# Attention outputs turned in 32x32 blocks on VectorE instead of whole on TensorE, with the sum and the scaling on GpSimd

## The chip, the core and the metric

The kernel is one launch on one core of a Trainium2 chip. The metric is the device time of that launch in microseconds (us), as the median over several runs. The core's engines work side by side, each through its own list of instructions in order: TensorE (PE in the profile; its weight loads are PEld), VectorE (DVE), ScalarE (ACT), GpSimd (POOL) and SyncE (SP), which here does nothing but issue DMAs. They wait for each other on counting semaphores.

## The reference

The input x is (4, 2048, 256) in fp32: four batches of 2048 tokens. Between two expert layers stands windowed attention with 16 heads of 16 columns:

```
x = x + 0.5 * ffn(layernorm(x))
x = x + attention(layernorm(x))          # |q - k| <= 128, or q == 0, or k == 0
x = x + 0.5 * ffn(layernorm(x))

attention:  softmax(q k^T / 4, masked) v, heads joined, @ Wo^T
ffn:        top-2 of 8 experts; an expert whose token count exceeds
            capacity 1280 contributes nothing
```

With these inputs every expert exceeds its capacity, so that the kernel computes the routing counts, finds no expert to run, and skips both expert layers. What is timed is the attention over all four batches and the routing.

## The kernel before, in words

**Tiles.** A batch is 16 tiles of 128 tokens; its 16 heads are 4 head groups of 4 heads. A group (16 tiles x 4 heads) is the outer unit: 16 groups, n = 0 to 15, four for each batch. A *step* is one tile of one group, 256 in all; a *quarter* is one head of a step. `stages` gives every piece of work a quarter number, `schedule` makes one list of events from these, and each engine walks the same list in order, doing its own events. The constants `QK_AT`, `OUT_AT`, `LATE_AT`, `MAX_AT` and the like are those quarter numbers. No planner is involved; the order is fixed when the kernel is built.

**What a quarter does.** Event A (L934): TensorE multiplies queries and keys over the window into one of three PSUM banks `a_ring`; VectorE (L1431) adds the mask and takes the row maximum. Event B runs 20 steps behind A: TensorE multiplies again with the maxima subtracted (L962), ScalarE takes the exponential into `probs` (L1105), GpSimd zeroes the two corners of the band (L1218, L1223, event CUT), and TensorE multiplies by the values (L980, event PV) into the bank `o_bank`.

**Stacks.** Queries and keys are split in three bf16 pieces (`pieces`, L1055, L1070, L1206). For each group and each quarter of its tiles (chunk c = 0 to 3) SyncE issues 12 DMAs, STACK (L718, L721), which place the pieces in `q_stack` and `k_stack`. TensorE's A event of tiles 0, 3, 7 and 11 waits until the stack of chunk 0, 1, 2, 3 has landed:

```
if h == 0 and t in (0, 3, 7, 11):
    i = 4 * g + (t + 1) // 4
    pe.wait_ge(stack_sem(i), stacked(i))
```

`pieces` has two buffers: ScalarE's first piece of chunk i (L1053) waits for the landing of the stack of chunk i - 2.

**The end of a group.** After its last tile the maxima are turned and split (TURN_MAX, MAX, PIECES), and SyncE issues 3 DMAs (MAX, L727) which put them in `q_stack`. GpSimd (P0, L1195) and ScalarE (EXP0, L1095) compute `p0`, the weight of key 0 for every query. With group n ending at quarter 64(n+1), the DMAs of SyncE are put at: MAX +2, STACK of the next group's chunk 2 at +11, of chunk 3 at +27, and those of the group after it, chunk 0 at +43 and chunk 1 at +59 (batches 1 to 3; the first batch has its own numbers).

**The outputs.** `o_bank` holds for four tiles (a quartet) the sums with heads on partitions (head h at partitions 32h, 17 columns of values and weight sum) and tokens in the row. There are 64 quartets. ScalarE copies it to `o_raw` (COPY_OUT, L1122; VectorE, L1352, for the last six), TensorE turns it by 16 small matmuls against columns of the identity (TURN, L1000), VectorE adds the term of key 0 in PSUM (OUT_ADD, L1460), takes reciprocals (L1467) and multiplies into `attn` (L1478), tokens on partitions. The term of key 0, `glob_term`, is made by GpSimd (GLOB, L1235).

**The projection.** For each quarter of a batch (LATE), TensorE turns the rows of `attn` by transposes of 128x128 (TURN_ATTN, L792), in two halves; ScalarE copies them to `attnT` (L1046; VectorE, L1344, in the last batch), and TensorE multiplies by Wo (PROJECT, L806).

Of the kernel before, what the change touches and what calls it, by code (L numbers as in the profile page):

```python
# [7 lines left out]
ALU = mybir.AluOpType  # L8
# [5 lines left out]
H, HD = 16, 16  # L14
# [34 lines left out]
def build(nc, x, wqk, wback, wv, wo, gate, w1, b1, w2, b2, consts, x1, out):  # L49
    ctx = ExitStack()  # L50
    with ctx:
        def sb(name, shape, dt=FP32):
# [28 lines left out]
        v0_all = sb("v0_all", [P, H * VW])  # L81
        o_raw = sb("o_raw", [P, 4 * P])
        glob_term = sb("glob_term", [P, 4, HG, VW])
        recip = sb("recip", [P, 4, HG])
        s0T = sb("s0T", [P, NT, H])
        row_max = sb("row_max", [P, 2, HG, NT])
        p0_arg = sb("p0_arg", [P, NT, HG])
        p0 = sb("p0", [P, 2, NT, HG])
# [12 lines left out]
        o0_norm = sb("o0_norm", [1, H, HD])  # L101
# [6 lines left out]
        attn_flat = attn[:, :, :].rearrange("p t d -> p (t d)")  # L108
        probs_flat = probs[:, :, :, :].rearrange("p a h n -> p (a h n)")
# [6 lines left out]
        o0_row = arena[0:1, 512:512 + H * VW]  # L116
# [4 lines left out]
        take = ident.rearrange("p (h c) -> p h c", c=SP)[:, :, 0:VW]  # L121
# [22 lines left out]
                 "glob_ready", "o_added", "recip_ready", "stored", "stored0", "stored1", "stored2",  # L144
# [248 lines left out]
        LATE = {'LOAD': -6, 'TURN_ATTN': 1, 'PROJECT': ((7, 8, 10, 10), (12, 12, 14, 14)),  # L393
                'BASE': 0, 'MOMENTS': (12, 17, 19, 21), 'RSTD': 23, 'STORE': 19}
        OUT_AT = (0, 0, 3, 3, 0, -1, -1, 0, 2, -1, 1, 0, 0, 0, 3, 4)
        OUT = {'TURN': 0, 'ADD': 0, 'RECIP': 1, 'MULT': 1}
        MAX_AT = {'KEY0': -1, 'TURN_MAX': 1, 'MAX': 2, 'PIECES': 3, 'P0': -1, 'EXP0': 6}

        def stages(nb, first):
# [22 lines left out]
            for i, (phase, b, c, at) in enumerate(order):  # L422
                plan = EARLY if phase == "EARLY" else LATE
                end(at + plan["LOAD"] if b or phase == "LATE" else -96, "LOAD", i)
                if phase == "LATE":
                    for p in range(2):
                        begin(at + LATE["TURN_ATTN"], "TURN_ATTN", i, p)
                        opening(at + LATE["TURN_ATTN"] + 1, "TURN_ATTN_IN", i, p)
# [20 lines left out]
            for n in range(NG * nb):  # L449
# [21 lines left out]
                opening(at + MAX_AT["EXP0"], "EXP0", n)  # L471
                for q in range(4):
                    at = 4 * LAG_TURN + GROUP * n + 16 * q + OUT_AT[4 * g + q]
                    begin(at + OUT["TURN"], "TURN", 4 * n + q)
                    end(at + OUT["ADD"], "OUT_ADD", 4 * n + q)
                    end(at + OUT["RECIP"], "OUT_RECIP", 4 * n + q)
                    end(at + OUT["MULT"], "OUT_MULT", 4 * n + q)
# [38 lines left out]
        FILLS = ("XT", "TURN_ATTN", "PROJECT", "QK", "TURN_MAX", "TURN", "VALUES", "FIRST", "FOLD")  # L516
        PARTED = ("PROJECT", "QK", "VALUES", "FIRST")
        EMPTIED = {"XT_IN": "XT", "TURN_ATTN_IN": "TURN_ATTN", "PROJECT_IN": "PROJECT", "REST": "QK", "PIECES": "TURN_MAX",
# [46 lines left out]
        def attend(nb, dram, batch_at, tiles_at, first):  # L565
# [42 lines left out]
            def drained(kind, n):  # L608

                if kind == "COPY_OUT":  # L610
                    return 4 * n + 3 + LAG_PV > NT * NG * nb
# [969 lines left out]
```

## Time and profile before

| | us |
|---|---|
| median of 3 runs | 870.6 |
| lowest, highest | 869.64, 871.29 |
| profiled execution, first to last instruction (span) | 867.2 |
| busy: TensorE matmul, its weight load | 814.6, 606.9 |
| busy: VectorE, ScalarE, GpSimd | 758.3, 637.2, 488.1 |
| mean granted TensorE clock, share of full | 0.997 |

The profile is of one execution; besides its span no time of its own is recorded. The profile counts an engine as busy in the union of its instructions. Matmuls overlap each other, so that the start of one to the start of the next is shorter than either lasts. SyncE has no busy time in the page: its DMA issues stand in the timeline of its queue (SPq), where the length is the time for which the queue was held by the issue, and a separate figure tells when the data landed.

### The profile page before, as it was taken

What the parts mean: (1) busy time and instruction counts of PE and PEld (TensorE: products, weight loads), DVE (VectorE), ACT (ScalarE), POOL (GpSimd) and SP (SyncE); (2) the same over time, 40 slices, a digit from 0 to 9 for tenths busy, and PEclk for the clock granted to TensorE, in tenths of its full rate; (3) what the DMA queues carried; (4) which work ended last, traced back from release to release, by engine and by line L of the source; (5) the groups of instructions that cost most, each with busy time, mean ns of one, the idle gap of its engine ahead of it and who ended that gap; (6) DMA issues with size and microseconds to landing.
All of it is one profiled execution on the core that took longest, in us unless ns stands there. A gap on an engine that the chain in (4) does not pass through costs nothing. (4 is left out here: it accounts for less than half of the span.)

```text
span 867.2 us, 50607 instructions
## 1 busy us (share of the span) xinstructions
PE 814.6 (94%) x21504; PEld 606.9 (70%) x21505; DVE 758.3 (87%) x2819; ACT 637.2 (73%) x1417; POOL 488.1 (56%) x874
## 2 busy tenths in 40 slices
PE   9798999999999999999999999898999999999894
PEld 8555667767777777667778777666778777766572
DVE  7898899989887899998987899998988889998785
ACT  2268888897877667998877666898777766888850
POOL 3212556675555557765554465675554556656763
PEclk9999999999999999999999999999999999999998
DMA  7722224432212344441213335352222335220113
GB/s 231 116 81 75 67 73 121 135 88 70 77 62 96 111 146 119 120 127 62 89 51 101 106 105 161 108 131 71 74 73 68 106 93 149 94 77 18 49 51 102
DMA packets 93191, 83.51 MB, mean 96 GB/s; under 512 B 17568, under 2 KB 92192, under 8 KB 92960
## 3 DMA queue, kind: packets, MB, share of 16 engines
q1 hardware_dynamic: 91360, 78.91, 30.1%
q8 instruction: 171, 2.80, 1.5%
q10 hardware_dynamic: 1600, 1.31, 1.0%
q14 instruction: 60, 0.49, 0.2%
HBM read 20.66 MB, written 8.39 MB: 33 GB/s over the span
## 5 line engine op out<-in xcount | busy, mean ns | idle before, releaser
L1105 ACT ACTIVATE probs<-bank 128x384 f32<-128x384 f32 (+1 forms) x1024 | 462.8, 480 | 146.8 <-PE bank L962 137.4
L1431 DVE CUSTOM_DVE_ANT_0 bank<-bank,con 128x288 f32<-128x288 f32 x1024 | 494.4, 518 | 53.2 <-PE bank L934 44.8
L934 PE MATMUL bank<-k_stack,q_stack 96*32 96x288 bf16 x4096 | 325.4, 288 | 10.7 <-DVE row_max L1431 5.7
L962 PE MATMUL bank<-q_stack,k_stack 99*32 99x288 bf16 (+2 forms) x4096 | 319.8, 285 | 16.0 <-ACT probs L1105 9.7
L980 PE MATMUL bank<-probs,v_sb 128*32 128x128 f32 x5888 | 305.4, 272 | 3.6 <-issue 1.5
L1218 POOL TENSOR_SCALAR_AFFINE_SELECT probs<-probs 128x512 f32<-128x512 f32 x240 | 154.8, 645 | 180.1 <-ACT probs L1105 179.5
L980 PEld LDWEIGHTS bank<-probs,v_sb 128*32 128x32 f32 x5888 | 192.1, 110 | 36.7 <-issue 5.3
L962 PEld LDWEIGHTS bank<-q_stack,k_stack 99*32 99x32 bf16 x4096 | 123.6, 95 | 79.7 <-ACT probs L1105 53.5
L934 PEld LDWEIGHTS bank<-k_stack,q_stack 96*32 96x32 bf16 x4096 | 127.3, 95 | 74.0 <-DVE row_max L1431 21.3
L1223 POOL TENSOR_SCALAR_AFFINE_SELECT probs<-probs 128x512 f32<-128x512 f32 x240 | 154.1, 642 | 19.3 <-ACT probs L1105 19.2
L823 PE MATMUL bank<-xnT,wqk_sb 128*32 128x256 f32 x2048 | 158.1, 379 | 0.6 <-DVE neg_max L1453 0.5
L1431 DVE DVE_READ_ACCUMULATOR2_ANT row_max<- 128x1 f32 x1024 | 144.1, 141 | 0.0
L1206 POOL TENSOR_TENSOR pieces<-rest,pieces 128x512 bf16<-128x512 f32 x64 | 74.4, 1162 | 61.7 <-ACT pieces L1070 61.5
L838 PE MATMUL bank<-wv_sb,xnT 128*32 128x272 f32 x1024 | 83.9, 393 | 1.7 <-ACT v_sb L1077 1.1
L806 PE MATMUL bank<-wo_sb,attnT 128*32 128x264 f32 x1024 | 72.0, 386 | 1.9 <-DVE x_ring L1339 0.9
L823 PEld LDWEIGHTS bank<-xnT,wqk_sb 128*32 128x32 f32 x2048 | 64.6, 110 | 5.6 <-ACT v_sb L1077 1.2
L1055 ACT ACTIVATE pieces<-bank 128x512 bf16<-128x512 f32 x64 | 38.3, 599 | 20.7 <-PE bank L823 19.5
L1359 DVE TENSOR_TENSOR rest<-bank,pieces 128x512 f32<-128x512 f32 x64 | 44.1, 688 | 4.3 <-ACT pieces L1055 4.1
L1266 DVE BATCH_NORM_STATS2 stats<-x_ring 128x6 f32<-128x256 f32 x112 | 47.1, 421 | 0.2
L1000 PE MATMUL bank<-con,o_raw 128*32 128x68 f32 x2048 | 44.4, 223 | 2.6 <-issue 1.7
L1070 ACT ACTIVATE pieces<-rest 128x512 bf16<-128x512 f32 x64 | 40.6, 635 | 8.0 <-DVE rest L1359 7.8
L806 PEld LDWEIGHTS bank<-wo_sb,attnT 128*32 128x32 f32 x1024 | 33.2, 109 | 13.4 <-issue 2.2
(126 smaller groups left out, 737.2 us busy)
## 6 DMA issues: line engine op xcount, KB each, us to landing
q_stack<-pieces SPq DMA_DIRECT2D x384, 64.0 KB, 2.7
k_stack<-pieces SPq DMA_DIRECT2D x364, 64.0 KB, 2.7
x_ring<-in_x SPq DMA_DIRECT2D x28, 512.0 KB, 4.5
out_x<-x_ring SPq DMA_DIRECT2D x16, 512.0 KB, 3.9
attn<-in_x SPq DMA_DIRECT2D x4, 512.0 KB, 6.0
wback_sb<-in_wback SPq DMA_DIRECT2D x8, 256.0 KB, 6.0
k_stack<-pieces ACTq DMA_DIRECT2D x20, 64.0 KB, 3.6
q_stack<-neg_max SPq DMA_DIRECT2D x48, 16.0 KB, 2.3
```

What stands on the lines that cost most here:

```text
L806: last = pe.matmul(bank_of("PROJECT", i, t)[SP * s:SP * (s + 1), 0:D + E], attnT[:, t // 2, k, at:at + SP], wo_sb[:, k, :], start=(k == 0) ...
L823: last = pe.matmul(bank_of("QK", g, c)[SP * s:SP * (s + 1), 256 * half:256 * (half + 1)], wqk_sb[:, g % NG, k, SP * s:SP * (s + 1)], xnT[: ...
L838: last = pe.matmul(bank_of("VALUES", b, t)[SP * s:SP * (s + 1), 0:D + HD], xnT[:, k, at:at + SP], wv_sb[:, k, :], start=(k == 0), stop=(k ...
L934: last = pe.matmul(a_ring[i % len(a_ring)][SP * s:SP * (s + 1), 0:WIN], q_stack[g % 2][0:KROWS, h, q:q + SP], k_stack[g % 2][0:KROWS, h, q ...
L962: last = pe.matmul(b_ring[i % len(b_ring)][SP * s:SP * (s + 1), start:final], k_stack[g % 2][0:SROWS, h, WINDOW + P * j + SP * s:WINDOW + ...
L980: last = pe.matmul(o_bank[SP * h:SP * (h + 1), P * (i % 4):P * (i % 4 + 1)], v_sb[:, j, VW * head:VW * head + SP], probs[:, j % 4, h, P * ...
L1105: act.activation(probs[:, j % 4, h, c0:c1], b_ring[i % len(b_ring)][:, c0:c1], ACT.Exp, scale=LOGIT_SCALE).then_inc(S["exp_ready"], 1)
L1206: pool.tensor_tensor(pieces[i % 2][:, 2, :], rest[:, :], pieces[i % 2][:, 1, :], ALU.subtract).then_inc(S["piece3_ready"], 1)
L1218: pool.affine_select(out=part, in_=part, compare_op=ALU.is_ge, fill=0.0, base=0, pattern=[[0, HG], [1, P]], channel_multiplier=-1).then_in ...
L1223: pool.affine_select(out=part, in_=part, compare_op=ALU.is_ge, fill=0.0, base=0, pattern=[[0, HG], [-1, P]], channel_multiplier=1).then_in ...
L1266: dve.bn_stats(stats[:, t, :], x_tiles(i)[:, t, :]).then_inc(S["stats_ready"], 1)
L1431: dve.tensor_tensor_reduce(out=a_ring[i % len(a_ring)][:, 0:WIN], in0=a_ring[i % len(a_ring)][:, 0:WIN], in1=mask, scale=1.0, scalar=con[: ...
```

## The change

1. `o_raw` is turned by VectorE, `dve.transpose`, in 32x32 blocks, into `o_turned` in SBUF (OUT_TURN, 58 of the 64 quartets). For the last six VectorE turns `o_bank` directly, and the copy goes. TensorE's TURN goes.
2. After a turn in blocks, partition 32h + r holds token r of each block of 32 for head h: heads stay on groups of 32 partitions. So `v0_all` (FIRST stage 6) and the first row (stage 8) are made in that layout, by four matmuls in place of one.
3. `p0` must be moved to the same layout. SyncE issues 16 DMAs of 32 partitions x 16 values for each group (P0_IN, at quarter +8 after the group's end), between MAX (+2) and the next STACK (+11). GLOB waits for these, and is put one step later, 36 quarters after the group's end.
4. OUT_ADD and OUT_MULT go to GpSimd (from SBUF); OUT_RECIP stays on VectorE, between them.
5. TensorE's TURN_ATTN and ScalarE's copy go: VectorE turns `attn`, in its new layout, straight to `attnT`, in 32x32 blocks. The rows of Wo are loaded in that order, by 4 DMAs in place of 1.

```diff
-        OUT = {'TURN': 0, 'ADD': 0, 'RECIP': 1, 'MULT': 1}
-        MAX_AT = {'KEY0': -1, 'TURN_MAX': 1, 'MAX': 2, 'PIECES': 3, 'P0': -1, 'EXP0': 6}
+        OUT = {'TURN': 0, 'ADD': 1, 'RECIP': 5, 'MULT': 6}
+        OUT_END = {'TURN': 0, 'ADD': 0, 'RECIP': 1, 'MULT': 1}
+        P0_MOVES = HG * P // SP
+        MAX_AT = {'KEY0': -1, 'TURN_MAX': 1, 'MAX': 2, 'PIECES': 3, 'P0': -1, 'EXP0': 6, 'P0_IN': 8}
...
-        LATE = {'LOAD': -6, 'TURN_ATTN': 1, 'PROJECT': ((7, 8, 10, 10), (12, 12, 14, 14)),
+        LATE = {'LOAD': -6, 'TURN_ATTN': (2, 5), 'PROJECT': ((7, 8, 10, 10), (12, 12, 14, 14)),
...
+                        elif kind == "P0_IN":
+                            g, = n
+                            sp.wait_ge(S["p0_ready"], g + 1)
+                            if g >= 2:
+                                sp.wait_ge(S["glob_ready"], 4 * (g - 1))
+                            for h in range(HG):
+                                for m in range(P // SP):
+                                    sp.dma_start(p0_heads[SP * h:SP * (h + 1), g % 2, m, :],
+                                                 p0[SP * m:SP * (m + 1), g % 2, h, :]).then_inc(S["p0_moved"], 16)
...
-                        elif kind == "TURN":
-                            n, = n
-                            pe.wait_ge(S["o_copied"], n + 1)
-                            claim(pe, "TURN", n)
-                            for i in range(4):
-                                for s in range(4):
-                                    at = P * i + SP * s
-                                    last = pe.matmul(
-                                        bank_of("TURN", n)[SP * s:SP * (s + 1), HG * VW * i:HG * VW * (i + 1)],
-                                        o_raw[:, at:at + SP], take, start=True, stop=True)
-                            last.then_inc(full_sem("TURN", n), 1)
...
+                        elif kind == "OUT_ADD":
+                            n, = n
+                            pool.wait_ge(S["o_turned"], n + 1)
+                            pool.wait_ge(S["glob_ready"], n + 1)
+                            sums = o_turned[:, :, :, 0:VW].rearrange("p t m c -> p (t m) c")
+                            pool.tensor_tensor(sums, sums, glob_term[:, :, :, :].rearrange("p t m c -> p (t m) c"),
+                                               ALU.add).then_inc(S["o_added"], 1)
+                        elif kind == "OUT_MULT":
...
+                            pool.wait_ge(S["recip_ready"], n + 1)
...
+                        elif kind == "TURN_ATTN":
...
+                            dve.transpose(attnT[:, p, :, :],
+                                          attn_heads[:, at:at + 8, :, :].rearrange("p b k e -> p k b e"))\
+                               .then_inc(S["attn_turned"], 1)
+                        elif kind == "OUT_TURN" and not drained(n[0]):
+                            n, = n
+                            dve.wait_ge(S["o_copied"], n + 1)
+                            if n:
+                                dve.wait_ge(S["out_ready"], n)
+                            dve.transpose(o_turned[:, :, :, :].rearrange("p t m c -> p (t m c)"), o_raw[:, :])\
+                               .then_inc(S["o_turned"], 1)
```

## Rows read from the trace of the kernel before

**Rows 1.** The page, busy time and share of the span of each engine.

```profile
PE 814.6 (94%) x21504; PEld 606.9 (70%) x21505; DVE 758.3 (87%) x2819; ACT 637.2 (73%) x1417; POOL 488.1 (56%) x874
```

**Rows 2.** Busy time by stretch: tile 7 to the end, of groups 8 to 11.

```profile
core 0: us, PE busy (x) PEld busy (x) DVE busy (x) ACT busy (x) POOL busy (x), PEclk, DMA share, GB/s
...
420.30:449.80 29.50, 29.50 (x821) 23.38 (x817) 25.17 (x93) 23.17 (x53) 15.97 (x25) 1.00 0.24 77
...
471.10:505.20 34.10, 34.09 (x893) 25.25 (x887) 28.46 (x105) 23.49 (x52) 17.60 (x33) 1.00 0.35 111
...
528.60:556.90 28.30, 25.66 (x740) 19.42 (x728) 26.52 (x108) 21.47 (x48) 20.41 (x39) 1.00 0.51 148
...
576.30:605.60 29.30, 26.02 (x800) 19.34 (x792) 24.80 (x97) 25.30 (x58) 17.50 (x30) 1.00 0.34 91
```

**Rows 3.** Timeline of SyncE's queue from group 7's MAX (start us, us held, what).

```profile
404.91 1.78 SPq L727 DMA_DIRECT2D q_stack<-neg_max  x3
406.79 1.08 SPq L718 DMA_DIRECT2D q_stack<-pieces  x1
407.91 0.59 SPq L721 DMA_DIRECT2D k_stack<-pieces  x1
408.55 0.59 SPq L718 DMA_DIRECT2D q_stack<-pieces  x1
...
416.38 0.59 SPq L718 DMA_DIRECT2D q_stack<-pieces  x1
```

**Rows 4.** The same queue: last DMA of chunk 2's stack, groups 9 to 11.

```profile
462.07 0.60 SPq L718 DMA_DIRECT2D q_stack<-pieces  x1
...
519.62 1.40 SPq L718 DMA_DIRECT2D q_stack<-pieces  x1
...
570.23 1.64 SPq L718 DMA_DIRECT2D q_stack<-pieces  x1
```

**Rows 5.** Timeline of TensorE: A of tile 7, groups 8 to 11, and one TURN.

```profile
420.27 0.30 PE L934 MATMUL bank<-k_stack,q_stack 96*32 96x288 bf16 x4
...
420.68 0.66 PE L1000 MATMUL bank<-con,o_raw 128*32 128x68 f32 x32
421.16 0.31 PE L934 MATMUL bank<-k_stack,q_stack 96*32 96x288 bf16 x4
...
471.15 0.33 PE L934 MATMUL bank<-k_stack,q_stack 96*32 96x288 bf16 x2
...
528.58 0.29 PE L934 MATMUL bank<-k_stack,q_stack 96*32 96x288 bf16 x4
...
576.27 0.30 PE L934 MATMUL bank<-k_stack,q_stack 96*32 96x288 bf16 x4
```

**Rows 6.** DMAs of the page, with median us from issue to landing.

```profile
q_stack<-pieces SPq DMA_DIRECT2D x384, 64.0 KB, 2.7
...
out_x<-x_ring SPq DMA_DIRECT2D x16, 512.0 KB, 3.9
```

**Rows 7.** Line L733, the stores: ns held, minimum/median/maximum, and starts.

```profile
L733 SPq DMA_DIRECT2D out_x<-x_ring x16: 383/390/1317, 291.7 to 858.7; - x16
```

**Rows 8.** Timeline of ScalarE: EXP0 of group 7.

```profile
406.53 0.25 ACT L1095 ACTIVATE p<-p_arg 128x64 f32<-128x64 f32 x1
```

**Rows 9.** Groups of instructions: count, busy us, mean ns of one, idle before.

```profile
L1206 POOL TENSOR_TENSOR pieces<-rest,pieces 128x512 bf16<-128x512 f32 x64 | 74.4, 1162 | 61.7 <-ACT pieces L1070 61.5
...
L1000 PE MATMUL bank<-con,o_raw 128*32 128x68 f32 x2048 | 44.4, 223 | 2.6 <-issue 1.7 <-ACT o_raw L1122 0.9
...
L1235 POOL TENSOR_TENSOR glob_term<-v_all,p 128x272 f32<-128x272 f32 x64 | 41.4, 647 | 1.8 <-DVE v_all L1400 1.8
...
L1460 DVE TENSOR_TENSOR bank<-bank,glob_term 128x272 f32<-128x272 f32 x64 | 29.2, 456 | 10.2 <-PE bank L1000 9.1
...
L1478 DVE TENSOR_TENSOR attn<-bank,recip 128x256 f32<-128x256 f32 x64 | 27.2, 425 | 3.3
...
L792 PE MATMUL bank<-con,attn 128*128 128x128 f32 x128 | 17.4, 279 | 0.8 <-DVE attn L1478 0.3
...
L1352 DVE COPY o_raw<-bank 128x512 f32<-128x512 f32 x6 | 4.1, 687 | 5.4 <-PE bank L980 5.4
```

More of the change, by code:

```diff
@@ L471, in stages @@
                 opening(at + MAX_AT["EXP0"], "EXP0", n)
+                end(at + MAX_AT["P0_IN"], "P0_IN", n)
                 for q in range(4):
                     at = 4 * LAG_TURN + GROUP * n + 16 * q + OUT_AT[4 * g + q]
[L474 to L477, printed above, removed]
+                    plan = OUT if n < NG * nb - 1 else OUT_END
+                    opening(at + plan["TURN"], "OUT_TURN", 4 * n + q)
+                    end(at + plan["ADD"], "OUT_ADD", 4 * n + q)
+                    end(at + plan["RECIP"], "OUT_RECIP", 4 * n + q)
+                    end(at + plan["MULT"], "OUT_MULT", 4 * n + q)
             for b in range(nb):
@@ L515, in build @@
         FIRST_PARTS = (4, 4, 4, 1, 1, 1, 1, 4, 1)
[L516 removed]
+        FILLS = ("XT", "PROJECT", "QK", "TURN_MAX", "VALUES", "FIRST", "FOLD")
         PARTED = ("PROJECT", "QK", "VALUES", "FIRST")
[L518 to L519 removed]
+        EMPTIED = {"XT_IN": "XT", "PROJECT_IN": "PROJECT", "REST": "QK", "PIECES": "TURN_MAX",
+                   "VALUES_IN": "VALUES", "FIRST_IN": "FIRST", "FOLD_IN": "FOLD"}
         def schedule(nb, first):
@@ L542, in schedule @@
                     events.append(("CUT", b))
[L543 removed]
+                q, turn = divmod(k + 2 - LAG_TURN, 4)
                 if turn == 0 and 0 <= q < items // 4:
@@ L899, in _ @@
                                 claim(pe, "FIRST", b, stage)
-                                last = pe.matmul(m[:, 0:H * VW], ones[0:1, :], v_sb[0:1, 0, 0:H * VW],
-                                                 start=True, stop=True)
+                                rows = v_heads[0:1, 0, 0:H, :].rearrange("p (g h) c -> p g h c", h=HG)
+                                for h in range(HG):
+                                    last = pe.matmul(m[SP * h:SP * (h + 1), 0:NG * VW], ones[0:1, 0:SP], rows[:, :, h, :],
+                                                     start=True, stop=True)
                             elif stage == 7:
@@ L914, in _ @@
                                 claim(pe, "FIRST", b, stage)
-                                last = pe.matmul(m[0:1, 0:H * VW], ones[:, 0:1], masked_o0,
-                                                 start=True, stop=True)
+                                rows = masked_o0.rearrange("p (g h c) -> p g h c", h=HG, c=VW)
+                                for h in range(HG):
+                                    last = pe.matmul(m[SP * h:SP * (h + 1), 0:NG * VW], ones[:, 0:SP], rows[:, :, h, :],
+                                                     start=True, stop=True)
                             if part == FIRST_PARTS[stage] - 1:
@@ L1116, in _ @@
                             act.activation(wide[1], wide[0], ACT.Exp).then_inc(S["route_exp"], 1)
-                        elif kind == "COPY_OUT" and not drained(kind, n[0]):
+                        elif kind == "COPY_OUT" and not drained(n[0]):
                             n, = n
```

174 lines of the change are left out of this document (72 added, 102 removed).

## Prediction

> **What bounds the kernel now.** I read the page first. TensorE is busy 94% of the span, VectorE 87%, ScalarE 73%, GpSimd 56% [rows 1]. No engine is idle long enough to say at once what an edit is worth, so I went to the busy time by stretch. In the second part of a group (tile 7 to the next group's start), group 8 and group 9 have TensorE busy in every microsecond (29.5 of 29.5, 34.1 of 34.1) with VectorE at 25.2 and 28.5; in group 10 VectorE leads (26.5 of 28.3, TensorE 25.7); in group 11 three engines are close (TensorE 26.0, VectorE 24.8, ScalarE 25.3 of 29.3) [rows 2]. So TensorE sets the pace in half of the loop and shares it in the rest. Relief of TensorE alone is worth something, but VectorE is close behind.
>
> The engines are not all there is. SyncE's queue has its own timeline. From MAX on it issues DMA behind DMA: starts at 407.91 and 408.55 are 0.64 us apart, of which the queue is held 0.59 [rows 3], and there are 12 of them for each stack, 48 for a group; one group takes about 51 us (A of tile 7 starts at 420.27 and, a group later, at 471.15 [rows 5]). Some issues take longer: the first of chunk 2's stack starts at 406.79 and the last, held for 0.59, at 416.38, 10.2 us for twelve against 7.6 at 0.64 each [rows 3]. What the stacks are for, and when, is the next thing to see. Chunk 2's stack of group 8 is issued last at 416.38, lands 2.7 us after that by the median [rows 3, 6], at 419.1, and A of tile 7, which waits for it, starts at 420.27 [rows 5]. The spare is 1.2 us. For groups 9, 10 and 11, reckoned in the same way (2.1 us from the end of the issue to the landing): landed 464.8, 523.1, 574.0, needed 471.15, 528.58, 576.27, spare 6.4, 5.5 and 2.3 [rows 4, 5, 6]. The mean of four is 3.9 us. This queue is the hidden third bound: it costs nothing now, and it has little left.
>
> **The change, part by part.**
>
> *TensorE* loses TURN and TURN_ATTN. One TURN is 0.66 long, but the next matmul starts 0.48 after it [rows 5]; 64 of these are 31 us. TURN_ATTN is 17.4 busy in all [rows 9], taken whole. Together 48 us (62 if the busy time of TURN, 44.4, were taken [rows 9]). The new FIRST stages add 6 small matmuls for a batch, nothing against that.
>
> *VectorE* loses OUT_ADD 29.2 and OUT_MULT 27.2 [rows 9] and 14 copies of 0.69 (six of o_raw, eight of attnT, priced by the former's row), 9.6: 66 us. It gains 58 + 6 + 32 = 96 turns of 128x512. The trace has no turn on VectorE. The nearest row is a copy of the same size, 0.687 [rows 9], and I take it: 66 us. Bounds: no cheaper than the smaller OUT_MULT, 0.425 (25 us less); at the dear end a turn that takes two passes, 1.37 (66 us more). Net nothing: VectorE stays at 758.
>
> *ScalarE* loses 24 copies of attnT, a little under 0.7 each, some 16 us. It leads nowhere in rows 2, so this is hidden.
>
> *GpSimd* gains 64 adds of 128x272 at 0.647 (its GLOB is that shape) and 64 products of 128x256, half of its 1.162 for 512 columns or 0.6 [rows 9]: 41 + 38 = 79, which makes 567 of 867 us. It has 8 to 16 us idle in each stretch of rows 2, so the work itself is hidden. What is not quite hidden is the order: VectorE's reciprocal now waits for GpSimd's add, and whatever A follows it on VectorE waits too. The add stands 4 quarters, about 3 us, ahead of it, behind two band cuts. I price this at 0 and bound it by one add each, 64 x 0.65 = 41 us.
>
> *SyncE* gains 16 moves of p0 for each group, and this is the step that decides. They wait for EXP0, which ends at 406.8 [rows 8], just when MAX's three issues end (404.91 + 1.78) [rows 3]: no further wait, but no gap to hide in. Then 16 issues at 0.64 are 10.2 us. Behind them in the same queue is the stack of chunk 2, with a spare of 1.2 to 6.4 us. It lands 10.2 later; A of tile 7 comes 10.2 - 3.9 = 6.3 us late in the mean. TensorE works in order, so nothing behind that A runs, B and its exponentials stop with it, and VectorE, 87% busy, has no A to do. MAX of this group comes as much later, so that the next group meets the same delay again: it doesn't amortise. It happens to 15 groups (the last one's moves have no stack behind them, and GLOB, 28 quarters after them, is not reached): 15 x 6.3 = 95 us. In the first batch the stacks have other places; I take the same mean.
>
> The price of one issue is bounded below by the cheapest DMA this queue shows, a store of median 0.390 [rows 7], plus the 0.04 between issues: 6.9 for 16, 3.0 late, 45 us in all. Above, by what the twelve of group 8 took, long issues included, 10.2/12 = 0.85: 13.6, 9.7 late, 146 us. I take 0.64, as the moves touch few bytes, and bytes don't seem to matter (those cheapest stores have 512 KB [rows 6]).
>
> The Trainium skill, page "DMA: Bandwidth & Descriptors", section "Anatomy of one DMA", lists the sequencer's dispatch of a DMA (there for those that GpSimd issues) at about 50 ns. By that the 16 moves would cost an estimated 0.8 us, under every spare above, and the whole term would be zero. The rows of this queue hold 0.59 for nearly each DMA, so I follow them; that rule is the fast rival below.
>
> *What TensorE's relief is worth beside it.* Work saved ahead of tile 7 only makes the wait for the stack longer. In the part after tile 7, three of a group's four TURNs are saved, 1.4 us, and in the second group of a batch four halves of TURN_ATTN as well, 4 x 0.54 = 2.2. Where TensorE alone leads (groups 8, 9) all of it counts, where it shares (10, 11) half: 1.4 + 3.6 + 0.7 + 0.7 = 6.4 for a batch, 25 for four.
>
> *Sum.* 867.2 + 95 - 25 = 937 us of span. The median of the runs is 3.4 above the span of the profiled execution, so 941 us.
>
> **The rivals.**
>
> *The moves are hidden* (other side). If an issue of such a small move is cheap, every stack lands in time. Then TensorE's relief counts before tile 7 too: per batch 1.9 + 4.1 in the two groups that it leads, and half of 1.9 + 2.2 and of 1.9 in the others, 9 us, 36 for four: 835. The deciding point: the late A costs nothing on balance while 16 moves take less than the spare, 3.9, plus 25/15 = 1.7 us, that is 0.35 us a move. For it: all rows of 0.59 are of two kinds of DMA, MAX and STACK [rows 3], and may owe it to their shapes. Against it: no DMA of this queue, of any shape, is under 0.383 [rows 7].
>
> *Turns on VectorE are dear, or its reciprocal waits for GpSimd*, on top of the late stacks. Two-pass turns add 66 us of VectorE's time; in the stretches where it has 3 to 5 us of room most of it vanishes, in those like group 10's it doesn't; I count half, 33: 974.
>
> *Hidden moves, dear turns or waits.* 835 plus 33: 868, no measurable change. It needs two things at once.
>
> *ScalarE stalls earlier than TensorE.* Its first piece of the next group's chunk 0 reuses the buffer of chunk 2 and waits for the same landing; in the second and third group of a batch it is placed 3 to 5 quarters ahead of A of tile 7. At 0.8 us a quarter (50.9/64) this adds up to 3 us in half of the groups: 15 to 20 us, 959. It is inside the range and not in the sum, since ScalarE has room.
>
> *The change doesn't do what it says.* TensorE's turns are gone from its list for certain; there is no such rival.
>
> **How the numbers follow.** Late stacks as summed, with the bounds of the issue price (891 to 992) and of ScalarE: 0.72. Late stacks with dear turns or waits: 0.14. Moves hidden, TensorE's relief kept: 0.10. Both small: 0.04. The predicted time is the first, 941. The range of 8 in 10 is 885 to 985: it leaves out the hidden moves and the far end of the dear cases. Runs of this kernel agree within about 0.2%, so a change below that can't be told from none: slower by more 0.87, within it 0.03, faster by more 0.10.
>
> **What would show it.** Right: SyncE's queue shows 16 issues of p0_heads at about 0.64 right behind each MAX; TensorE's A (L934 before) waits for the DMA of k_stack or q_stack, some 6 us, 15 times; from one A of tile 7 to the next it takes some 5 us more; GpSimd near 567 busy, VectorE near 758, both with a lower share. Wrong in the first step if the moves are held under 0.35 each or TensorE doesn't wait for stacks; wrong in the price of a turn if VectorE's transposes are far from 0.69; wrong in the order if VectorE's reciprocal shows idle time ended by GpSimd's add.

## The result, and the profile after

The changed kernel takes 1003.0 us by the median (999.18 to 1004.25), the kernel before 870.1 on the same chip: a ratio of 1.151, 95% interval 1.147 to 1.155. The profiled execution has a span of 997.6 us against 867.2. The forecast was 941, with a range of 885 to 985: right in direction and in the main mechanism, 62 us too low and outside the range.

The busy line of the page after and its row of granted clock in 40 slices (before in [rows 1]):

```profile
PE 810.3 (81%) x19376; PEld 570.3 (57%) x19377; DVE 753.8 (76%) x2785; ACT 627.2 (63%) x1393; POOL 574.2 (58%) x1002
...
PEclk9899898999797997989799898988989799897998
```

No engine has more to do in a way that could matter: VectorE has 4.5 us less, GpSimd 86 more and is still idle 42% of the span. All shares fell, TensorE's from 94% to 81%. The time went into gaps in which everything stands. SyncE's queue after, from group 7's MAX on (start, us held, what; before in [rows 3]):

```profile
467.77 1.89 SPq L737 DMA_DIRECT2D q_stack<-neg_max  x3
469.76 11.49 SPq L746 DMA_DIRECT2D p_heads<-p  x16
481.35 0.59 SPq L728 DMA_DIRECT2D q_stack<-pieces  x1
...
488.66 0.59 SPq L728 DMA_DIRECT2D q_stack<-pieces  x1
```

The sixteen moves stand between MAX and chunk 2's stack, as forecast, and hold the queue for 11.5 us. TensorE in the same stretch (in brackets: idle before, and what ended it; before in [rows 5]), and the busy time of all engines in slices of 5 us (columns as in [rows 2]):

```profile
482.45 0.60 PE L829 MATMUL bank<-xnT,wqk_sb 128*32 128x256 f32 x8
491.29 0.43 PE L944 MATMUL bank<-k_stack,q_stack 96*32 96x288 bf16 x4 [8.24 <-DMA q_stack<-pieces]
```

```profile
480.00:485.00 5.00, 2.92 (x72) 1.70 (x72) 3.86 (x17) 3.16 (x8) 3.30 (x6) 1.00 0.17 52
485.00:490.00 5.00, 0.00 (x0) 0.00 (x0) 0.00 (x0) 0.00 (x0) 0.47 (x1) 0.62 0.29 101
490.00:495.00 5.00, 3.71 (x60) 2.55 (x64) 1.72 (x7) 1.30 (x3) 0.00 (x0) 0.50 0.32 105
495.00:500.00 5.00, 5.00 (x112) 3.39 (x108) 4.25 (x17) 4.04 (x9) 3.12 (x5) 0.86 0.22 72
500.00:505.00 5.00, 5.00 (x148) 4.10 (x142) 4.15 (x16) 4.27 (x11) 2.97 (x6) 1.00 0.26 85
```

The list of waits names the same cause, once on ScalarE and once on TensorE, with the total in us, the count and the longest; the third row is the wait that was bounded by 41 us and priced at nothing:

```profile
ACT pieces L1045 <- DMA q_stack<-pieces: 70.7, 10, 9.4
...
PE bank L944 <- DMA q_stack<-pieces: 64.7, 8, 10.6
...
DVE recip L1487 <- POOL o_turned L1236: 6.5, 6, 1.8
```

Last, the groups of instructions that are new or moved (count, busy us, mean ns of one, idle before):

```profile
L1236 POOL TENSOR_TENSOR o_turned<-o_turned,glob_term 128x272 f32<-128x272 f32 x64 | 45.9, 718 | 2.5 <-DVE o_turned L1372 2.4
...
L1247 POOL TENSOR_TENSOR attn<-o_turned,recip 128x256 f32<-128x256 f32 x64 | 41.5, 648 | 21.3 <-DVE recip L1487 20.9
...
L1372 DVE STREAM_TRANSPOSE o_turned<-o_raw 128x512 f32<-128x512 f32 x58 | 41.0, 707 | 1.4 <-ACT o_raw L1112 1.2
...
L1364 DVE STREAM_TRANSPOSE attnT<-attn 128x512 f32<-128x512 f32 x32 | 22.3, 698 | 0.3
```

**Where the 130 us of span are.** From each trace I took, for the 15 groups with a next one, the time from the first issue of MAX to the A of tile 7, and from there to the next MAX; beside them the first A, the four batches (from a batch's first A to the next batch's) and what follows the last A. For these last three the mark is VectorE's instruction of event A, some 0.5 us behind TensorE's, so the first A stands 0.5 us later in the table than in the rows of TensorE. For group 7 after, the first is 467.8 to 491.3, 23.5 us; before it was 404.9 to 420.3, 15.4 [rows 3, 5].

| kernel | first A at | batches 1 to 4 | MAX to A of tile 7, sum | A of tile 7 to MAX, sum | tail |
|---|---|---|---|---|---|
| before | 26.9 | 175.1, 200.4, 203.1, 190.6 | 257.3 | 474.0 | 71.1 |
| after | 31.9 | 198.0, 235.3, 235.3, 224.7 | 366.4 | 487.9 | 72.5 |
| e1_no_moves | 30.6 | 178.9, 197.5, 196.4, 185.5 | 254.9 | 462.7 | 72.2 |
| e2_moves_alone | 27.0 | 204.2, 242.0, 242.3, 233.9 | 373.2 | 509.6 | 70.6 |
| e3_half_moves | 31.3 | 190.1, 212.3, 212.5, 205.0 | 302.2 | 478.4 | 71.3 |
| e5_bounce_wo_late | 26.9 | 182.5, 198.1, 196.8, 187.2 | 253.4 | 472.7 | 72.4 |
| e7_kept_busy | 31.0 | 200.4, 238.5, 236.3, 230.5 | 393.1 | 473.2 | 72.5 |
| e9_kept_fit | 33.3 | 201.3, 232.0, 233.3, 224.6 | 369.5 | 481.1 | 71.3 |
| e10_one_wo | 26.9 | 181.2, 197.3, 199.1, 188.5 | 254.6 | 471.9 | 72.0 |
| e11_back_late | 27.7 | 175.9, 197.0, 196.7, 185.4 | 253.9 | 463.6 | 74.7 |

After less before: +109.1 from MAX to A, +13.9 from there to MAX, +5.0 ahead of the first A, +1.4 in the tail, together 129 of 130. The 109 fall on 13 of the 15. In the first and third group of the first batch the moves stand behind chunk 2's stack and the stop comes at chunk 3 instead: 36.1 and 36.0 where before had 30.5 and 30.5. That is 11 of the 13.9, so all stops together are 120 us, 8.0 for each of 15.

### The profile page after: what moved, and what is told of

Same layout as the page of the kernel before. It is cut to its first block and busy times, and to the rows that moved or that the text cites. A ratio compares the mean times of both kernels' runs of the same rounds, so it can differ in the third digit from the quotient of the medians.

```text
span 997.6 us, 46656 instructions
## 1 busy us (share of the span) xinstructions
PE 810.3 (81%) x19376; PEld 570.3 (57%) x19377; DVE 753.8 (76%) x2785; ACT 627.2 (63%) x1393; POOL 574.2 (58%) x1002
## 5 line engine op out<-in xcount | busy, mean ns | idle before, releaser
L944 PE MATMUL bank<-k_stack,q_stack 96*32 96x288 bf16 x4096 | 329.6, 300 | 89.3 <-DMA q_stack<-pieces 64.7
L972 PE MATMUL bank<-q_stack,k_stack 99*32 99x288 bf16 (+2 forms) x4096 | 326.7, 296 | 69.0 <-ACT probs L1095 64.6
L990 PE MATMUL bank<-probs,v_sb 128*32 128x128 f32 x5888 | 314.0, 281 | 9.4 <-POOL probs L1212 5.3
L829 PE MATMUL bank<-xnT,wqk_sb 128*32 128x256 f32 x2048 | 162.6, 389 | 0.6 <-DVE neg_max L1482 0.5
L844 PE MATMUL bank<-wv_sb,xnT 128*32 128x272 f32 x1024 | 88.7, 412 | 1.6 <-ACT v_sb L1067 1.1
L812 PE MATMUL bank<-wo_sb,attnT 128*32 128x264 f32 x1024 | 74.4, 402 | 3.4 <-DVE attnT L1364 2.1
L1247 POOL TENSOR_TENSOR attn<-o_turned,recip 128x256 f32<-128x256 f32 x64 | 41.5, 648 | 21.3 <-DVE recip L1487 20.9
L1060 ACT ACTIVATE pieces<-rest 128x512 bf16<-128x512 f32 x64 | 40.5, 633 | 12.9 <-DVE rest L1386 12.8
L1236 POOL TENSOR_TENSOR o_turned<-o_turned,glob_term 128x272 f32<-128x272 f32 x64 | 45.9, 718 | 2.5 <-DVE o_turned L1372 2.4
```

Of the source, the lines that this page charges most:

```text
L812: last = pe.matmul(bank_of("PROJECT", i, t)[SP * s:SP * (s + 1), 0:D + E], attnT[:, t // 2, k, at:at + SP], wo_sb[:, k, :], start=(k == 0) ...
L829: last = pe.matmul(bank_of("QK", g, c)[SP * s:SP * (s + 1), 256 * half:256 * (half + 1)], wqk_sb[:, g % NG, k, SP * s:SP * (s + 1)], xnT[: ...
L844: last = pe.matmul(bank_of("VALUES", b, t)[SP * s:SP * (s + 1), 0:D + HD], xnT[:, k, at:at + SP], wv_sb[:, k, :], start=(k == 0), stop=(k ...
L944: last = pe.matmul(a_ring[i % len(a_ring)][SP * s:SP * (s + 1), 0:WIN], q_stack[g % 2][0:KROWS, h, q:q + SP], k_stack[g % 2][0:KROWS, h, q ...
L972: last = pe.matmul(b_ring[i % len(b_ring)][SP * s:SP * (s + 1), start:final], k_stack[g % 2][0:SROWS, h, WINDOW + P * j + SP * s:WINDOW + ...
L990: last = pe.matmul(o_bank[SP * h:SP * (h + 1), P * (i % 4):P * (i % 4 + 1)], v_sb[:, j, VW * head:VW * head + SP], probs[:, j % 4, h, P * ...
```

## The experiments

Four questions were put: is it the moves, and all of it (e1, e2, e3)? Can they be had more cheaply or elsewhere (e4, e6, e12)? What else does the change cost (e5, e8, e10)? What is lost behind a stop (e7, e9)? The times that open each measurement are medians; ratios are to the kernel before on the same chip (872.1 us for e1 to e4, 871.6 for e5 to e8, 871.9 for e9 to e12), with 95% intervals. Spans, windows and sums by group come from one profiled execution of each kernel.

### e1_no_moves: the change without the moves

```diff
-                end(at + MAX_AT["P0_IN"], "P0_IN", n)
...
+                            pool.memset(p0_heads[:, :, :, :], 0.0).then_inc(S["p0_moved"], 1)
...
-                            pool.wait_ge(S["p0_moved"], 16 * P0_MOVES * (g + 1))
+                            pool.wait_ge(S["p0_ready"], g + 1)
```

> The changed kernel without its 256 moves of p0: GpSimd reads a block of zeros in their place, so the term of key 0 is left out of the sums; every other instruction stays. Late stacks (my theory): SyncE's queue is as free as before, no A waits for a stack, TensorE's clock stays full, and the time falls from 1003 to 840 to 865 us (835 for TensorE's relief, plus the 5 us by which the first A came later). Rival, the work on GpSimd and VectorE and the waits between them cost the time: it stays above 960 us.

Measured: 866.6 us against 872.1, ratio 0.993 (0.990 to 0.996), 1.6 above the range. The span is 861.1. All the added time hangs on the moves: from e1 to after they cost 136.5 us of span. The rest of the change helps, by 6 us rather than the 25 to 36 that I had reckoned. Its page and the windows of tile 7 to the next group, groups 8 to 11 (before in [rows 2]; these start and end at TensorE's A, so they are up to 1.1 us shorter at the end):

```profile
PE 782.6 (91%) x19376; PEld 558.7 (65%) x19377; DVE 749.0 (87%) x2785; ACT 624.5 (73%) x1393; POOL 573.0 (67%) x1003
```

```profile
424.70:452.00 27.30, 27.30 (x703) 20.25 (x699) 23.69 (x86) 22.61 (x53) 19.20 (x30) 1.00 0.25 83
473.60:505.10 31.50, 30.13 (x754) 20.74 (x749) 28.22 (x104) 21.15 (x48) 20.57 (x36) 1.00 0.35 115
529.10:555.20 26.10, 23.91 (x608) 16.53 (x609) 24.98 (x101) 20.23 (x44) 22.82 (x42) 1.00 0.51 152
575.70:602.20 26.50, 23.46 (x677) 16.94 (x673) 23.03 (x88) 24.43 (x56) 21.18 (x36) 1.00 0.31 88
```

TensorE leads in the first window only, full; in the second it now has 1.4 us idle with VectorE at 28.2 of 31.5. By the page TensorE's busy time fell 32 us (814.6 to 782.6), where I had taken 48.

### e2_moves_alone: the kernel before, plus the moves

Nothing reads the moved data.

```diff
+        p0_heads = sb("p0_heads", [P, 2, P // SP, NT])
...
+                end(at + MAX_AT["P0_IN"], "P0_IN", n)
...
+                            for h in range(HG):
+                                for m in range(P // SP):
+                                    sp.dma_start(p0_heads[SP * h:SP * (h + 1), g % 2, m, :],
+                                                 p0[SP * m:SP * (m + 1), g % 2, 4 * h:4 * h + 4, :].rearrange("p t h -> p (t h)")).then_inc(S["p0_moved"], 16)
```

> The kernel before with the 16 moves for each group added at the same place of SyncE's queue, into a buffer that nothing reads; nothing else of the change. Late stacks: the moves hold the queue for 11.7 us a group against a mean spare of 3.9, so 15 x 7.8 = 117 us and some 2 us a group for the half clock after each stop: 990 to 1025 us. Rival, the moves are not what costs: below 890 us.

Measured: 1021.4 us, ratio 1.168 (1.162 to 1.174), inside the range; span 1019.9: the moves alone cost 153 us. The waits are those of the changed kernel:

```profile
PEld bank L946 <- DMA q_stack<-pieces: 68.4, 8, 10.9
ACT pieces L1067 <- DMA q_stack<-pieces: 68.1, 10, 9.5
```

By the table the 153 are 115.9 from MAX to A, 35.6 from A to MAX (15.8 of it stops at chunk 3, 38.4 twice against 30.5; 19.8 spread over the other stretches), and 1 elsewhere. The stops are 132, 8.8 for each of 15, and 20 are lost *behind* them. Sixteen moves take 12.1 us here in the mean of the 15 groups, so the spare that the stops leave is 3.3. Given the moves, the rest of the change takes 22 us off (997.6 against 1019.9): 29 in the batches, less 7 ahead of the first A and in the tail. Of the 29, 6.8 lie from MAX to A of tile 7 (373.2 against 366.4), where the stack sets the time and not TensorE.

### e3_half_moves: eight moves a group

Heads 2 and 3 are not moved.

```diff
-                            for h in range(HG):
+                            for h in range(2):
```

> The changed kernel with the moves of two of the four heads only, 8 a group; the other two heads' key 0 term is zero. Late stacks: 8 moves hold the queue for 5.9 us, which is 2 over the mean spare and less than the spare in half of the groups, so most of the 15 stops shrink to 0 to 5 us: 880 to 915 us, much nearer to the kernel without moves than halfway. A cost in proportion to the moves would give some 925.

Measured: 923.0 us, ratio 1.058 (1.053 to 1.063), outside the range and near the 925 that I had named for a cost in proportion to the moves. The expectation came from my forecast's arithmetic: 8 moves less a spare of 3.9 should leave little. They hold the queue for 5.74 us in this row of the queue's timeline, and chunk 2's stack starts 7.7 us behind MAX in that group, where it started 1.9 behind it before [rows 3], 5.8 later:

```profile
438.08 5.74 SPq L746 DMA_DIRECT2D p_heads<-p  x8
```

The span is 922.5, 55 over the kernel before. Of these, 45 us stand from MAX to A in the 15 groups (302.2 against 257.3) and 5.3 at one chunk 3 (35.8 against 30.5). The spare that these groups really have, delay of the queue less delay of A, is 2.2, 0.4, 5.6 and 2.1 for groups 8 to 11 (5.8 less 3.6, 5.4, 0.2 and 3.7), a mean of 2.6. Group 9, which I had given 6.4, has next to none. Its stop is on ScalarE. This is ScalarE's timeline in the changed kernel at the same group, where the wait is longer:

```profile
538.94 0.49 ACT L1095 ACTIVATE probs<-bank 128x384 f32<-128x384 f32 x1 [0.41 <-PE bank L972]
547.96 0.60 ACT L1045 ACTIVATE pieces<-bank 128x512 bf16<-128x512 f32 x1 [8.52 <-DMA q_stack<-pieces]
```

The first piece of the next group's chunk 0 waits for the landing that frees its buffer, 5 us ahead of A of tile 7 (552.9), and the exponentials queued behind it wait too. The second groups of batches 2 to 4 are alike in the changed kernel: MAX to A of tile 7 grew by 10.7, 10.0 and 10.9 us in groups 5, 9 and 13, no less than where TensorE itself waits, though the stack that TensorE needs had over 5 us of spare there before.

### e4_bounce: one DMA out to DRAM, four back

```diff
+        MAX_AT = {'KEY0': -1, 'TURN_MAX': 1, 'MAX': 2, 'PIECES': 3, 'P0': -1, 'EXP0': 6, 'P0_IN': 8, 'P0_BACK': 12}
...
+                            sp.dma_start(p0_dram[g % 2, :, :, :].rearrange("p h t -> p (h t)"),
+                                         p0[:, g % 2, :, :].rearrange("p h t -> p (h t)")).then_inc(S["p0_out"], 16)
...
+                            by_head = p0_dram[g % 2, :, :, :].rearrange("(m r) h t -> h r m t", r=SP)
                             for h in range(HG):
+                                sp.dma_start(p0_heads[SP * h:SP * (h + 1), g % 2, :, :], by_head[h])\
+                                  .then_inc(S["p0_moved"], 16)
```

> The changed kernel with p0 moved through DRAM: one DMA of all 128 partitions out, ahead of the stack of chunk 2, and four DMAs back (one for each head), behind that stack. 5 issues a group for 16, of which only one (0.7 us) stands before the urgent stack; the four (2.9 us) delay the stack of chunk 3, whose spare is 2.8 us at the least. Late stacks: 845 to 870 us, within 15 of the kernel without moves. Rival: above 960 us.

Measured: 877.0 us, ratio 1.005 (1.002 to 1.007), 7 above the range. SyncE's queue:

```profile
458.74 1.78 SPq L738 DMA_DIRECT2D q_stack<-neg_max  x3
460.77 0.38 SPq L745 DMA_DIRECT2D p_scratch<-p  x1
461.25 1.17 SPq L729 DMA_DIRECT2D q_stack<-pieces  x1
...
470.44 3.02 SPq L754 DMA_DIRECT2D p_heads<-p_scratch  x4
```

The same 32 KB cost the queue 0.4 us ahead of the stack in place of 11.5, and the stops are gone (253.5 from MAX to A). So it is the issues and not the bytes: five take 3.4 us in this group where sixteen took 11.7 in the mean, and four of the five stand behind the urgent stack. How much of the gain is their number and how much their place this run doesn't separate; e6 shows that the place alone isn't enough. What stayed above the expectation asked for something outside the groups, and the first A showed it (next run).

### e5_bounce_wo_late: e4, and Wo's four loads later

The change also loads Wo head by head in four DMAs of 64 KB, ahead of the first stack. Here they come at quarter 80.

```diff
-                        by_head = wo.rearrange("(g h c) k n -> h g c k n", g=2, h=HG)
-                        for h in range(HG):
-                            sp.dma_start(wo_sb[SP * h:SP * (h + 1), :, 0:D], by_head[h]).then_inc(S["wo_in"], 16)
...
+                end(80, "WO_IN")
```

> The kernel with p0 moved through DRAM (877 us), and the four loads of Wo issued at quarter 80 in place of before the first stack. Each of them has a slowest dimension of 2 and so, by my reading, few DMA engines work on 256 KB just when the first stack is to land; the first A came 3.7 to 5 us later in every kernel with these loads, and not in the kernel before. If so, the first A is back at 27 us and the time falls by 4 to 7: 870 to 873 us. Rival, the new layout's first matmuls or VectorE's work in the opening delay it: no change, 877.

Measured: 870.6 us against 871.6, ratio 0.9995 (0.997 to 1.002), inside the range. The first A of TensorE in the timelines of after and of this run (e4, which differs from this run in the loads alone, has it at 30.93):

```profile
31.29 0.67 PE L944 MATMUL bank<-k_stack,q_stack 96*32 96x288 bf16 x8 [7.35 <-DMA k_stack<-pieces]
```

```profile
26.40 0.55 PE L954 MATMUL bank<-k_stack,q_stack 96*32 96x288 bf16 x8 [2.01 <-DMA k_stack<-pieces]
```

Four loads placed ahead of the first stack make it land 4.5 to 5 us late. The queue isn't what delays it: the first issue of that stack starts at 16.52 after and at 16.48 before. It is the data that lands later. The forecast has no term for them: I had read the diff's DMAs inside the loop and not those ahead of it.

### e6_moves_behind: the moves behind chunk 2's stack

```diff
-        MAX_AT = {'KEY0': -1, 'TURN_MAX': 1, 'MAX': 2, 'PIECES': 3, 'P0': -1, 'EXP0': 6, 'P0_IN': 8}
+        MAX_AT = {'KEY0': -1, 'TURN_MAX': 1, 'MAX': 2, 'PIECES': 3, 'P0': -1, 'EXP0': 6, 'P0_IN': 12}
```

> The changed kernel with its 16 moves at quarter +12 in place of +8, behind the stack of chunk 2. If only the place in the queue counts, chunk 3's stack (spare 2.8 to 10 us) is now 11.7 us late: stops of 2 to 9 us, some 6 in the mean, 950 to 985 us. If the queue is short of time in all (some 70 DMAs at 0.73 us are 51 us, as long as a group), moving them about gains little and the time stays above 980.

Measured: 971.2 us, ratio 1.115 (1.109 to 1.120), inside the range. From MAX to A is 252.4 now, as without moves; from A to MAX 570.1, 96 more than before. TensorE waits as long at a time, at the next chunk:

```profile
PE bank L944 <- DMA q_stack<-pieces: 49.4, 12, 11.9
```

Neither of the two places tried has 11 us free: 48 stack issues and 3 for MAX already take 33 of a group's 51 us at 0.64 each, and more with the long ones. Moves spread over several places of the group, a few at each, were not tried.

### e7_kept_busy: idle matmuls in the stops

Up to 30 matmuls of ones are put ahead of A of tile 7's wait, into a free bank of `a_ring`.

```diff
+        KEPT = (0, 0, 30, 0, 30, 0, 22, 28, 30, 0, 22, 28, 30, 0, 22, 28)
...
+                            if h == 0 and t == 7 and KEPT[g]:
+                                i = HG * n + h
+                                pe.wait_ge(S["a_free"], i - len(a_ring) + 1)
+                                for _ in range(KEPT[g]):
+                                    pe.matmul(a_ring[i % len(a_ring)][:, 0:P], ones[:, :], ones[:, :], start=True, stop=True)
```

> The changed kernel, with TensorE given 22 to 30 idle matmuls of 128x128 (some 6 to 8 us) ahead of the wait for chunk 2's stack in the ten groups where it stops there for 7 to 11 us. The stops stay as long. If the half clock behind each stop costs 2 to 3 us, as the longer stretches behind tile 7 say, the granted clock is back over 0.96 and the time falls by 15 to 30 us, to 973 to 990. If the clock costs nothing, since VectorE sets the pace behind a stop: no change, 1000 to 1005.

Measured: 1009.1 us, ratio 1.157 (1.152 to 1.162): missed, slower than the changed kernel. The mean granted clock rose from 0.922 to 0.948 and the stretches behind the stops shrank by 14.7, but those ahead grew by 26.7, of which 20 are in groups 6, 10 and 14 (26.8, 26.2 and 26.0 became 32.8, 32.8 and 33.2): there the idle matmuls came on top of the stop, as ScalarE's wait ends it and not TensorE's. These three groups hide what the clock does; e9 leaves them out.

### e9_kept_fit: the same, fitted to the stops

```diff
+        KEPT = (0, 0, 30, 0, 30, 0, 0, 24, 26, 0, 0, 26, 26, 0, 0, 30)
```

> e7_kept_busy again, with idle matmuls only in the seven groups whose stop stands at this wait in full (24 to 30 of them, 6.6 to 8.3 us); in e7_kept_busy those of groups 6, 10 and 14 came on top of the stop and cost 6 to 7 us each. In the others its groups were 1.2 to 2.6 us shorter than the changed kernel's. If that is the half clock: 7 x 2 = 14 us off 1003, 985 to 995. If it was chance: 1000 to 1005.

Measured: 1001.2 us, ratio 1.149 (1.144 to 1.154), which can't be told from the changed kernel's 1.151; it is the "chance" branch of the expectation. The mean clock is 0.946. The stretches behind the stops are 6.8 shorter, those ahead 3.1 longer, the first A is 1.4 later. The groups show more than the total. The first 5 us from A of tile 7 of group 8, in the changed kernel and in this one (columns as in [rows 2]):

```profile
491.29:496.29 5.00, 5.00 (x76) 3.26 (x80) 2.27 (x9) 2.15 (x5) 0.56 (x1) 0.50 0.31 103
```

```profile
493.44:498.44 5.00, 5.00 (x136) 3.92 (x136) 4.41 (x16) 4.01 (x9) 1.60 (x3) 1.00 0.31 104
```

At a granted clock of 1.00 TensorE gets through 136 matmuls in place of 76, and VectorE and ScalarE are at work at once. From A of tile 7 to MAX this group takes 32.7 us after, 30.2 here and 30.3 in e1, which has no stop. In the four treated groups that have the full clock in these first 5 us (2, 4, 7 and 8) the stretches sum to 125.3 after, 121.7 here and 122.0 in e1. In the three that have 0.66 to 0.68 (11, 12 and 15) it is 87.3, 85.4 and 84.0. So the half clock is what makes the stretch behind a stop longer. If that holds for all groups, it accounts for the 13 us that after loses there against e1, of the 136.5 that the moves cost. It wasn't gained, because the seven stretches ahead of these stops grew by 3.1 (169.8 against 166.7) while those behind shrank by 5.5 (207.1 against 212.6), and the first A came later.

### e8_vector_sums: e5, with OUT_ADD and OUT_MULT on VectorE

```diff
-                            pool.tensor_tensor(sums, sums, glob_term[:, :, :, :].rearrange("p t m c -> p (t m) c"),
+                            dve.tensor_tensor(sums, sums, glob_term[:, :, :, :].rearrange("p t m c -> p (t m) c"),
```

(and the product in the same way).

> The kernel of e5_bounce_wo_late with the add of key 0's term and the product by the reciprocals on VectorE again (from SBUF), in the same places of the order; GpSimd loses them. VectorE gains 64 x (0.45 + 0.42) = 56 us and no longer waits for GpSimd's add (6.5 us in all). If VectorE shares the pace, as rows of before say (busy 87%), the time rises by a third to two thirds of that: 890 to 905 us. If TensorE still sets it alone: within 5 us of e5_bounce_wo_late.

Measured: 902.1 us, ratio 1.036 (1.032 to 1.039), inside the range; 31.5 us more than e5, for 55 us more of VectorE by its page (750.2 in e5):

```profile
PE 799.1 (89%) x19376; PEld 564.2 (63%) x19377; DVE 805.4 (89%) x2913; ACT 628.1 (70%) x1393; POOL 496.8 (55%) x874
```

More than half of what VectorE is given comes out as time: it is a bound of this loop as well as TensorE, so GpSimd's share of the work is worth having. Without it this kernel is 3.6% slower than the kernel before.

### e10_one_wo: e4, with Wo laid out by head on the host, one load

```diff
-                        for h in range(HG):
-                            sp.dma_start(wo_sb[SP * h:SP * (h + 1), :, 0:D], by_head[h]).then_inc(S["wo_in"], 16)
+                        sp.dma_start(wo_sb[:, :, 0:D], wo).then_inc(S["wo_in"], 16)
```

> p0 through DRAM (e4_bounce, 877 us), with Wo laid out in the order by heads in the launch's array, so that one DMA of 128 partitions loads it at its old place, as in the kernel before. The first A at 27 us in place of 31.5, without the four issues at quarter 80 that e5_bounce_wo_late had in the first batch (its groups 1 and 3 were 2.4 and 1.3 us longer than e4_bounce's): 4.5 us below e4_bounce and 2 to 4 below e5_bounce_wo_late, 866 to 870 us; before 871 to 872. Rival, these group lengths were chance: as e5_bounce_wo_late, 870 to 871.

Measured: 867.2 us against 871.9, ratio 0.996 (0.993 to 0.998), inside the range. The same bytes in one load leave the first A at 26.9; it was the form of the four loads, not their bytes or that they stand early. The 3.4 us between this median and e5's don't show in the profiled executions, whose spans are 864.9 and 863.9: a few us between two single profiles are not to be read.

### e11_back_late: e10, with the way back behind chunk 3's stack

```diff
-        MAX_AT = {'KEY0': -1, 'TURN_MAX': 1, 'MAX': 2, 'PIECES': 3, 'P0': -1, 'EXP0': 6, 'P0_IN': 8, 'P0_BACK': 12}
+        MAX_AT = {'KEY0': -1, 'TURN_MAX': 1, 'MAX': 2, 'PIECES': 3, 'P0': -1, 'EXP0': 6, 'P0_IN': 8, 'P0_BACK': 28}
...
-                q, turn = divmod(k + 2 - LAG_TURN, 4)
+                q, turn = divmod(k + 1 - LAG_TURN, 4)
```

> e10_one_wo with the four DMAs back behind the stack of chunk 3 (quarter +28) in place of chunk 2's, and GpSimd's term of key 0 one step later. The stack of chunk 3 is then not delayed, and the next one has 9 us of spare. If the 1.8 us for the four still cost something in e10_one_wo: 2 to 4 us less than it, 863 to 868. If they were hidden: the same. Rival, the term of key 0 is now late and holds GpSimd's band cuts: slower than e10_one_wo.

Measured: 862.2 us against 871.9, ratio 0.989 (0.986 to 0.993), just under the range: 1.1% faster than the kernel before, with an interval of 0.7 to 1.4%, and faster than the changed one. Its busy line and its queue:

```profile
PE 783.8 (91%) x19376; PEld 557.6 (65%) x19377; DVE 748.9 (87%) x2785; ACT 623.9 (73%) x1393; POOL 569.9 (66%) x1002
```

```profile
450.73 1.29 SPq L743 DMA_DIRECT2D p_scratch<-p  x1
...
470.00 3.07 SPq L752 DMA_DIRECT2D p_heads<-p_scratch  x4
```

The four issues no longer stand ahead of chunk 3's stack, and the term of key 0 comes one step later; the run doesn't separate the two. Against e10 the first batch gains 5.3 and the last 3.1. The last three batches are 15.0 shorter than before's: 5 each.

### e12_pool_moves: the sixteen moves on GpSimd

```diff
-                                    sp.dma_start(p0_heads[SP * h:SP * (h + 1), g % 2, m, :],
+                                    pool.dma_start(p0_heads[SP * h:SP * (h + 1), g % 2, m, :],
```

> The changed kernel with its 16 moves a group issued by GpSimd's queue in place of SyncE's, at the same place of the order. SyncE's queue is as before, so no A waits for a stack. GpSimd, busy 574 us, has some 15 us idle a group. If an issue holds it for about as long as it holds SyncE (0.7 us), the 11.7 us fit into that idle time only in part, as the band cuts behind them stand still: 890 to 950 us. If it holds it for 1 us or more: 950 to 1050. If for under 0.3: 860 to 875.

Measured: 969.8 us, ratio 1.113 (1.108 to 1.117), above the range. The line of the moves (ns held by an issue: least, median, most) and the waits of TensorE and VectorE for GpSimd:

```profile
L1229 POOL DMA_DIRECT2D p_heads<-p x256: 496/498/747, 75.9 to 892.3; - x128
```

```profile
PE bank L981 <- POOL probs L1203: 82.1, 23, 7.3
...
DVE recip L1487 <- POOL o_turned L1236: 53.6, 14, 7.7
```

Each issue holds GpSimd for 0.50 us, 8 us a group, and TensorE and VectorE wait for its band cuts and adds. Against e1 the moves cost 103 us here and 136 on SyncE's queue (969.8 and 1003.0 less 866.6); other engines stop for them.

## Why the prediction came out as it did

**SyncE's queue as the hidden bound: right.** The moves stand behind MAX, TensorE and ScalarE wait for the landing of `q_stack`, in 15 groups, and it doesn't amortise. Without the moves the time is gone (e1), the moves alone bring it all (e2), one issue ahead of the stack in place of sixteen removes it (e4). The sign that I gave, TensorE waiting some 6 us for a stack 15 times, came out otherwise: it waits 8 times, 8.1 us in the mean, and in the second and third groups of batches 2 to 4 it finds the stack landed, since ScalarE's wait for the same landing has held everything ahead of it.

**The step that failed is the size of "15 x 6.3 = 95".** The moves alone cost 153 (e2): 15 x 8.8 of stops and 20 behind them. Three parts of that term were off. *The price of an issue*: nearly every one holds the queue for 0.59, but the long ones count as they do for the stacks. Sixteen took 11.1 to 12.8 us, a mean of 11.7 or 0.73 each, where I took 0.64 and kept 0.85 as the bound. With 11.7 and the spare of 3.9 the sum is 15 x 7.8 = 117, and the stops measured are 120; in e2, where nothing but the moves differs, it is 12.1 less 3.3, and 132. *The spare* of 3.9 held in the mean at this delay, and that is luck: group 8 had 3.4 where I reckoned 1.2, group 9 had 1.5 where I reckoned 6.4. Where ScalarE's piece waits ahead of TensorE's A (the rival "ScalarE stalls earlier", which I had left out of the sum because ScalarE has room) the stretch grew by 10.0 us in group 9, not by 11.5 less 6.4, and by as much in groups 5 and 13. With half the moves the mean spare was 2.6 and the same arithmetic was far off (e3). *Behind the stop*: I let the work go on at its usual pace from the landing. But TensorE comes back at a granted clock of 0.50, the lower of its two levels (1.2 GHz), and VectorE and ScalarE, which live on what it delivers, are busy for 2.27 and 2.15 of the first 5 us. e2 loses 20 us there, and from e1 to after it is 13 (25.2 from A to MAX, of which 11.8 are chunk 3's stops). e9 shows that this is the clock: in the four groups that had the full clock behind the stop the stretch is as short as without a stop.

**TensorE's relief, -25: about right given the moves, but in part by luck, and too high without.** After less e2 is -29 in the batches. 6.8 of these lie ahead of tile 7, where I had given it nothing, and there the queue was held 0.4 us less a group by the same sixteen moves (11.7 for 12.1). Without stops it is smaller: e1 is 15 us shorter than before in the last three batches, 5 each where I had 9, and 4 longer in the first. TensorE's busy time fell 32, not 48, and VectorE soon leads (e8). Of these 4, 3 lie in the first group, 39.7 us long against 36.8: in e1 it starts 3.6 us late and at a granted clock of 0.50, before at 1.00. In e11, whose first A is 0.9 us late at the full clock, the first group takes 37.0 and the batch is within 1 us of before's. That the late first A costs these 3 us as well is likely and not shown by a run of its own.

**Not seen: the first A, +5.** Wo's four loads, shown by e5 and e10.

With these the sum is 58 more for the moves (153 for 95), 4 more relief in the batches (29 for 25) and 7 ahead of the first A and in the tail, +61 on 937, or 998. That it meets the 997.6 measured is no test, since the terms are differences between the spans of before, e2 and after.

**VectorE's turn** taken as a copy of the same size, 0.687: measured 0.698 to 0.707, VectorE 754 for 758. Two passes, the dear end, are out. **GpSimd** 567: 574, its adds at 0.718 rather than 0.647 and its products at 0.648 rather than 0.6. **The reciprocal's wait** priced at nothing: 6.5 us in all, and e1, which has the same 6.5, is no slower than before.

**The fast rival** needed issues under 0.35 us; none was. Its rule was the 50 ns of dispatch that the Trainium skill ("DMA: Bandwidth & Descriptors", section "Anatomy of one DMA") gives for DMAs that GpSimd issues. The same table lists the generation of the descriptors in a row of its own, as small and variable, and my estimate of 0.8 us left that out. What an issue held in all was 0.591 us by the median on SyncE, and 0.498 on GpSimd itself (e12). The dispatch alone is no price of an issue here, and the measurement decides.

## What to carry to other kernels

Count the issues that an edit adds to a DMA queue, at what a run of issues there takes with its long ones (0.73 us each here), and set the sum against the spare in front of the next transfer that someone waits for, on every engine that waits for it, not only the one that leads. Add what TensorE loses at the lower clock behind each stop, here about 1 us for each of 15. Where many small blocks must change partitions, one DMA out to DRAM and a few back cost this kernel's queue 3.4 us in place of 11.7, and brought the change from 15% slower than before to 0.5% slower (e4); with Wo in one load and the way back behind chunk 3's stack it was 1% faster (e11). Read the loads ahead of the loop as carefully as those in it.

## What the runs showed of the hardware

- A DMA of 2 KB holds SyncE's queue as long as one of 64 KB: 0.591 us by the median against 0.59. One from SBUF to DRAM (32 KB) held it for 0.38 to 1.29 in the rows above.
- GpSimd's issues of the moves go from 0.496 to 0.747 us (e12), SyncE's from 0.551 to 1.761:

```profile
L746 SPq DMA_DIRECT2D p_heads<-p x256: 551/591/1761, 84.6 to 939.2; - x128
```

- Four loads of 64 KB from a strided layout made the stack behind them land 4.5 to 5 us later, though it was issued at the same time (16.52 against 16.48); one load of the same bytes didn't (e10). That few of the DMA engines carry the four is a guess that no run tested.
- After the stop of 8.24 us in group 8 TensorE comes back at a granted clock of 0.50. At 0.50 it did 76 matmuls in 5 us there, at 1.00 the same stretch of work did 136 (e9). Keeping it at work through seven of the stops moved the mean from 0.922 to 0.946 and the time by nothing that can be measured.
